# A two-layer transformer on one core: the light projection steps of layer 0 spread over the first 29 of 39 expert blocks

## The reference

```python
xn = _layernorm(x)
q, k, v = xn @ Wq.T, xn @ Wk.T, xn @ Wv.T
q = q * cos + rotate_half(q) * sin
k = k * cos + rotate_half(k) * sin
k_feat = elu(k) + 1.0;  q_feat = elu(q) + 1.0
memory = einsum('bhsd,bhse->bhde', k_feat, v)
...
# experts, on the same xn: top 2 of 8 per token
g = einsum('nd,efd->enf', xn, gate_proj);  u = einsum('nd,efd->enf', xn, up_proj)
eo = einsum('enf,edf->end', silu(g) * u, down_proj)
```

## Time and profile before

| | us |
|---|---|
| median of 3 runs | 1075.36 |
| lowest and highest | 1073.11, 1081.39 |
| the profiled execution | 1074.24 |
| its span, first to last instruction | 1072.3 |
| of it the first expert matmul to the last one, about | 89 to 267 |
| TensorE busy in 89 to 267 | 144.68 |
| ScalarE, VectorE, GpSimd busy there | 101.06, 90.58, 114.68 |

### The profile page before, as it was taken

How to read it: one execution, slowest core, us unless ns; L and a number is a source line. 1 busy time by engine, 2 the same in 40 slices (tenths; PEclk the granted TensorE clock), 3 DMA queues, 4 the chain that set the end, 5 groups by cost and what they waited for, 6 DMA issues and landing times. The chain is left out here.

```text
span 1072.3 us, 15783 instructions
## 1 busy us (share of the span) xinstructions
PE 866.9 (81%) x4924; PEld 551.0 (51%) x4924; DVE 586.2 (55%) x1296; ACT 423.6 (40%) x734; POOL 348.6 (33%) x265
## 2 busy tenths in 40 slices
PE   3825888787377889989999888657999999999991
PEld 3714877676011233444444345544666666666660
DVE  5595455453385987657766723393334434444435
ACT  2124564655043554774675574041222222222220
POOL 3175657567330000201110030043334344344321
PEclk9967799899556999999989988687999999999995
DMA  6321425334373222234233014449954533644317
GB/s 218 107 54 54 143 98 168 119 109 163 102 222 102 67 71 60 82 109 145 79 108 128 21 70 137 118 146 295 271 181 106 126 89 99 122 98 99 98 39 240
DMA packets 157346, 130.43 MB, mean 122 GB/s; under 512 B 63916, under 2 KB 138684, under 8 KB 157276
## 3 DMA queue, kind: packets, MB, share of 16 engines
q1 hardware_dynamic: 149788, 109.07, 34.5%
q0 software_dynamic: 7488, 20.46, 6.1%
HBM read 83.47 MB, written 46.01 MB: 121 GB/s over the span
## 5 line engine op out<-in xcount | busy, mean ns | idle before, releaser
L1453 DVE TENSOR_REDUCE b_negmax<-b_psM 128x1 f32<-128x512 f32 x256 | 162.8, 682 | 72.0 <-PE b_psM L1700 69.9
L1363 ACT ACTIVATE b_probs<-b_psE 128x512 f32<-128x512 f32 x256 | 138.8, 595 | 130.9 <-PE b_psE L1718 130.3
L1700 PE MATMUL b_psM<-b_kst,b_qst 96*128 96x512 bf16 x256 | 101.8, 443 | 37.5 <-DMA b_vst<-scratch_v 18.2
L1718 PE MATMUL b_psE<-b_qst,b_kst 98*128 98x512 bf16 x256 | 90.9, 419 | 20.9 <-ACT b_probs L1363 10.2
L2066 POOL DMA_INDIRECT scratch_ys<-d_y,put x39 | 39.6, 1016 | 129.3 <-ACT d_y L2098 127.9
L1718 PEld LDWEIGHTS b_psE<-b_qst,b_kst 98*128 98x128 bf16 x256 | 20.9, 99 | 112.0 <-ACT b_probs L1363 50.0
L2218 PE MATMUL d_psG<-d_w,d_xT 128*128 x156 | 76.6, 614 | 2.0 <-DVE d_xT L2117 1.6
L1727 PE MATMUL b_psV<-b_probs,b_vst 128*32 128x512 f32 x512 | 75.5, 664 | 3.0 <-ACT b_probs L1363 3.0
L1700 PEld LDWEIGHTS b_psM<-b_kst,b_qst 96*128 96x128 bf16 x256 | 24.6, 101 | 98.9 <-DVE b_negmax L1453 68.5
L2243 PE MATMUL d_psY<-d_w,d_hidden 128*128 x312 | 74.9, 383 | 0.0
L2226 PE MATMUL d_psU<-d_w,d_xT 128*128 x156 | 74.5, 600 | 0.0
(11 more groups left out here) (369 smaller groups left out, 1947.3 us busy)
## 6 DMA issues: line engine op xcount, KB each, us to landing
held<-scratch_parts SPq DMA_DIRECT2D x192, 64.0 KB, 3.1
scratch_parts<-a_part SPq DMA_DIRECT2D x12, 512.0 KB
b_qst<-scratch_parts SPq DMA_DIRECT2D x96, 64.0 KB, 2.2
b_kst<-scratch_parts SPq DMA_DIRECT2D x96, 64.0 KB, 2.2
scratch_parts<-b_part SPq DMA_DIRECT2D x24, 256.0 KB, 3.1
scratch_v<-a_v SPq DMA_DIRECT2D x4, 1024.0 KB, 4.5
b_vst<-scratch_v SPq DMA_DIRECT2D x16, 256.0 KB, 2.9
held<-scratch_ys SPq DMA_DIRECT2D x8, 512.0 KB, 6.8
```

Of the source, the lines that this page charges most:

```text
L1363: nc.scalar.activation(probs[k % PSLOTS][:, h, :], psE[h % 2][:, :], ACT.Exp, scale=float(HD) ** -0.5).then_inc(scores_used[h % 2], 1)
L1453: nc.vector.tensor_reduce(negmax[i][:, t, h:h + 1], psM[:, h % 2, :], AX_X, ALU.max, negate=True).then_inc(rows_used[h % 2], 1)
L1700: nc.tensor.matmul(psM[:, h % 2, :], qst[g][0:STACK, h, t * P:(t + 1) * P], kst[g][0:STACK, h, :], start=True, stop=True).then_inc(rows_re ...
L1718: nc.tensor.matmul(psE[h % 2][:, :], kst[g][0:STACKM, h, k * P:(k + 1) * P], qst[g][0:STACKM, h, :], start=True, stop=True).then_inc(score ...
```

## The change

The spacing of the light steps in the order list is worked out from a new constant, `AHEAD = BLOCKS - 10`, that is 29, where 36 stood. All 39 remaining light steps have then been given out after 116 slots, and none follows. Every engine's own part moves with the list. No instruction is added or removed.

```diff
 F0H = F0 // 2
+AHEAD = BLOCKS - 10
 XSLOTS = 4
...
-            while given < min(len(rest) * used // (4 * (BLOCKS - 3)), len(rest)):
+            while given < min(len(rest) * used // (4 * AHEAD), len(rest)):
                 order.append(rest[given])
                 given += 1
```

## The result

The changed kernel takes 1087.09 us (median of 8 runs) beside 1079.45 us for the kernel before on the same chips. The ratio is 1.0086, with a 95% interval of 1.0063 to 1.0110: slower by 9 us, clear of noise, and under 1%. (The ratio is not that of the two medians, which lie 7.6 us apart.) The profiled execution took 1086.26 us where that of before took 1074.24.

A forecast was written before the change was run, and what follows sets the result against it. The first stage was taken as bound by a serial chain of light attention steps, with expert blocks as TensorE's cover. Terms +1.8 +0.7 −4.3 +3.5 +5.2 −0.4 +1.1 +0.5 = +8.1 us on the 1075.36 us median gave 1083, range 1073 to 1091.

The forecast's parts named there:

- second half to value projection: From the keys' projection to the value projection: 1.8 us lost in batches 1 to 3, another 0.7 in batch 0.
- value projection to key transposes: Over four batches: 4.3 us gained at full clock by shorter gaps, 3.5 lost to half clock behind longer waits.
- key transposes to next second half: From key transposes round to the next keys' projection: cover lost, with small new waits, 5.2 us lost.
- first gate to first second half: Start of the stage up to batch 0's keys' projection: batch 0's first wait 0.4 us shorter.
- last memory steps and tail: Behind the last key transposes: the last batch's memory steps cost 1.1 us, GpSimd's gathers and puts 0.5.
- pattern B: Batches 1 and 3: an input transpose and a gate ahead of the first rotation; 2.25 us wait before the second half.
- Pattern A: Batches 0 and 2: a gate and a hidden transpose ahead of the first rotation; 1.45 us wait before the second half.
- Cover is lost faster than the chain shortens: The forecast itself, for the first stage's light steps and expert blocks: 1079 to 1088 us, chance 0.55.
- the reload that enters batch 1: Silu table load, 1.28 us, newly between batch 1's exponential and second rotation; by the skill's page 1.4 us more.
- rival 2: First stage: light chain and block cover shrink alike, −0.6 up to +3 us, 1074 to 1079 us; chance 0.22.
- Rival 3: Faster: half clock behind the value projections goes away, giving back 6 us or so, 1066 to 1073 us; chance 0.08.
- Rival 4: GpSimd becomes the bound in the burst, ScalarE holds block copies 8 us in all, 1089 to 1096 us; chance 0.15.

The follow-up runs named there:

- shift29: The changed kernel's spacing with every light step one slot later; 1077.67 us, ratio 0.9994 to the kernel before.
- step3_29: The changed kernel with the keys' rotation on VectorE directly behind the light step ahead of it, TensorE's order untouched; 1072.98 us, ratio 0.9953 to the kernel before.
- the glued kernels: Every odd light step directly behind the even one ahead, TensorE's order kept, at spacings of 36, 29 and 33; 1065.65, 1066.20 and 1065.17 us.
- warm29: The changed kernel with 10 unused matmuls ahead of each value projection and 20 ahead of each set of key transposes; 1082.24 us, ratio 1.0040 to the kernel before.
- glue36: The kernel before with every odd light step directly behind the even one ahead of it, TensorE's order kept; 1065.65 us, ratio 0.9866 to the kernel before.
- glue36_warm: glue36 with 8 unused matmuls ahead of each set of key transposes; 1059.12 us, ratio 0.9837 to the kernel before.

## Why the prediction was right, and where it was not

**Time and direction.** 1083 us was forecast, 8.1 us on the profiled execution; the stage lost 8.4 us, the ratio puts the whole at +9 us. The measured 1087.09 lies 4 us above 1083 because the kernel before itself took 1079.45 us in these runs, where the prediction started from 1075.36.

**Its terms**, as forecast and from the table's first two columns:

| | forecast | measured |
|---|---|---|
| second half to value projection (+1.8 and +0.7) | +2.5 | +2.2 |
| value projection to key transposes (−4.3 and +3.5) | −0.8 | +0.5 |
| key transposes to next second half | +5.2 | +4.3 |
| first gate to first second half | −0.4 | +0.7 |
| last memory steps and tail (+1.1 and +0.5) | +1.6 | +0.7 |

That the sum came out within 0.3 us is luck: four terms are off by 0.9 to 1.3 us, two each way. The step for batch 0's first wait failed: I had the rotation start sooner and forgot that a down projection and an input transpose (0.93 us) left the cover. The wait grew from 1.21 to 1.91 us. The last memory steps and the tail were priced at twice what they cost. The round to the next second half was 0.9 us too dear, of which 0.7 are its three waits (5.25 us, walked as 5.95). From value projection to key transposes the walk's full-clock length for pattern B holds (11.25 us, measured 11.18), and what was too small is the 3.5 us for half clock: the four sections take 48.8 us where the walk at full clock had 44.1, 4.7 more. Pattern A at full clock was never seen, so how that 4.7 divides is open for it.

**The waits.** Ahead of the second halves 1.45 us in pattern A and 2.25 in B were forecast; 1.21 (batch 2), 2.02 and 2.02 (batches 1 and 3) came. Ahead of the value projections "3 to 4 us" holds for A alone (3.33 and 3.28). In B it was 1.91 and 1.51: the section took 9.37 us, as walked (9.55), but part of the time went elsewhere, in batch 1 as 0.97 us ahead of a hidden transpose, which the walk did not have.

**The reason.** "Cover is lost faster than the chain shortens" is true of this order and false as a rule. The walk was right because it followed the two patterns through the queues, and it named the reload that enters batch 1. What it did not ask is what the other alignment of the same spacing would do: in shift29 chain and cover shrink almost alike (1.5 us lost for 12.8 us of blocks moved), which is rival 2's picture, with a time to match. The 8 us are thus mostly (6.9) the place where the steps land, and little (1.5) the ten blocks without them. This split is against the one alignment of the kernel before; its spacing was not tried at another.

**The rivals.** Rival 2's argument, that ScalarE's work in the queue goes along with the cover, is shown by step3_29, shift29 and the glued kernels; its time was wrong for this alignment. Rival 3, full clock behind the value projections: not so, the clock fell in three of them as before. Over the 5 us from their starts it was 0.69, 0.70, 0.50 and 1.00; in the kernel before 0.50, 0.69, 0.66 and 1.00, so only one of the three that the prediction called half clock was at it for all of that stretch. Rival 4, GpSimd: refuted, 4.7 us of ScalarE's waits instead of 5.7. (Behind the keys' `rest` of batch 3 stand five gathers, as the list shows, and not four: one is ahead of the last subtraction.) The last key transposes started at 244.63 us, where about 242 was forecast; 1.7 us of that is the stage's later start. The tail behaved as said: blocks at 2.1 us and once 2.7, no wait of TensorE over 0.7 us for a y copy.

**The table load.** With the drain that the Trainium skill's page ScalarE: Activation LUTs gives (What ACT_TABLE_LOAD costs) the sum would have been, as an estimate, +9.5. In batch 1 the Silu starts 0.01 us behind the end of its load here too (144.62 + 1.28, 145.91): the trace shows the load alone, as before. The measured +8.4 can't decide between the two sums, since single terms were off by as much as they differ.

**What stays open.** In shift29 about half a microsecond of the 3.0 us from value projection to key transposes, and 0.8 of the 1.7 us of the round to the next second half (the waits there are 0.9 us shorter), have no cause shown. Why the clock fell behind some waits and not behind others is open too.

## What to carry to other kernels

Where in-order engines walk one list, a spacing is not one number. Write out what stands ahead of each critical operation on its own engine, for each alignment: here one slot was worth 7 us, and the planned change of the spacing cost 1.5 at one alignment and 8.4 at another. Before thinning or thickening the filler, take the chain's operations ahead of the filler on the engines that carry the chain; that left TensorE's order alone, was worth 15 us of the stage, and made the spacing nearly free. Price a wait with the half clock behind it, not by its length alone.

## What had not been expected of the hardware

The clock's share: 30 matmuls a batch that compute nothing, put into waits that were there anyway, shortened a stage by 7.1 us (warm29), and 8 a batch another by 2.9 us (glue36 to glue36_warm, clock 0.93 to 0.97). The half clock does not follow the length of the wait directly ahead alone: in the changed kernel waits of 3.33 and 1.91 us ahead of value projections have it behind them, and 1.51 us ahead of the last has not; before, 1.77 had it and 1.91 had not the earlier trace rows.
